# Mixing stage: whole-chunk scans with zeroed tile heads, and the ternary products in two exact passes

## The chip, the cores and the metric

The kernel runs on one core of a Trainium2 chip. The metric is the device time of one launch in microseconds (us). Five engines work side by side, each in its own order and tied by semaphores: PE (TensorE, matmuls and transposes into PSUM), ACT (ScalarE), DVE (VectorE), POOL (GpSimd) and SP, which only issues DMAs.

## The reference

Input `x` is 4 sequences of 1024 tokens with 256 channels, all in fp32. Three blocks follow one another: attention with 16 heads and a residual; a ternary feed-forward (layer norm, then a product with a weight rounded to -1, 0 or 1 and a scale); and a memory that is updated by gradient steps along the tokens, with a gate, and a second ternary feed-forward behind it. What matters here is how the memory's state runs over the tokens of a chunk of 128 tokens (in the kernel: a *tile*):

```
k, v, q = causal convolutions of four taps over projections of hidden
alpha, eta, theta = gates per token, means over 64 features
within each tile of 128 tokens, g from the state at the tile's start:
    S = eta[t] * S - theta[t] * g[t]
    W = (1 - alpha[t]) * W + S
ternary feed-forward: y = normalised(x) @ round_to_-1_0_1(w / scale) * scale
```

The recurrence is linear, so inside a tile it is written as four running sequences of factors, and each begins anew at a tile's first token. These four are the scans: `fz` (product of the etas, in the upper 64 partitions), `E` (eta times the former value minus the identity's column), `ab` (keep times the former value plus `fz`) and `C` (keep times the former value plus `E`), where keep is 1 - alpha.

## The kernel before, in words

Three stages run one after the other: projections and attention up to about 782 us of the profile's span, the *mixing* stage up to about 983 us, and the *memory* stage (`remember`) to the end. The change is in the mixing stage (`mix`), with small edits of buffers and one wait in the memory stage.

The mixing stage works on 8 chunks of 512 tokens (4 tiles of 128). It is a pipeline written out by hand: an iteration `it` from -4 to 7 does different steps for the chunks `it` to `it + 4`, and every engine walks its own fixed order of steps in each iteration:

- PE: projections of chunk it+1 (`projections`, L1244), ternary products of it+2 (`ffn_products`, L1181), gate means of it+1 (L1250), turning `z` of it+3 (`turn_z`, L1187), turning and multiplying keys of `it` (`key_products`, L1258 and L1264), gate products of it+1 (L1181), theta of it+1 (L1272), turning `hid` of it+2 (`turn_h`, L1187), attention output products of it+4 (`out_products`, L1181). The three L1181 groups share one helper, `token_products`: per chunk 8 products of 128x128 by 128x256, each of which the profile shows as two matmuls in fp32, so 16 rows. They share the two halves of one PSUM tile `ps_a`; `turn_z` and `turn_h` share `ps_t`.
- DVE: `add_out` of it+3 (L1103, with the moments L69 and L73), taps 1 and 2 of the convolution of `it` (L1134), `put_z` of it+3 (L81), tap 3 of `it`, `add_ffn` of it+2 (L1117, moments), `scan_decays` of `it` (the `fz` and `E` scans, L1146 and L1147, per tile), `put_h` of it+2 (L81), `scan_keeps` of `it` (the `ab` and `C` scans, L1081 and L1082, and four small copies L1087 to L1090), `products_of_keys` of `it` (L1095, tile `G`).
- ACT: copies of the projections of it+1 (L972 to L984), oldest taps (L998), log-sigmoid (L1003, behind a table load), `means` (eta L1010 and keep L1012), then the copy `zT` of it+3 out of `ps_t` (L1045), keys and values of `it` (L1029 to L1033), gates of it+1 (L1039), theta (L1018), the copy `hT` of it+2 (L1051).
- POOL: at the stage's start three clears (L940, L942) and ten clears of the memory stage's tiles (L951); in each iteration the deviations (L99 and L101), `divide_heads` of it+5 (L516), and the terms `aqb` and `kce` of `it` (L931 and L935).
- SP: loads of heads, stores of the terms; then it goes on with the memory stage's loads (L1387, L1394), the first of which wait for the last chunk's theta and for stored terms. `load_chain(1)` fills the second set of buffers.

Waits that matter: `out_products(n)` waits until the gates of chunk n-3 have left `ps_a`; `turn_h(n)` waits for `hid` of n and for the `zT` copy of n+1, since both use `ps_t`; `theta` waits for `keep`, since it writes over the means in PSUM; `gate_means` waits for the sigmoid L982. The last chunk's `ab` and `C` scans are left to the memory stage.

Of the kernel before, what the change touches and what calls it, by code (L numbers as in the profile page):

```python
# [795 lines left out]
Mix = namedtuple("Mix", ("on_sync on_gpsimd on_scalar on_vector on_tensor stored last_terms memory_terms scan_keeps products_of_keys pre sig_ea sig_t vT kce zT hT G aqb kv_c q_c eta keep ab C_ z hid ps_p ps_t ps_a states_zeroed th_ready f_ready gates_ready gate_ready th_taken hT_ready gate_taken g_ready kv_taken"))  # L796
# [3 lines left out]
def mix(ctx, nc, const, cols, oT, inverse, heads, x_all, gate_all, mem, states):  # L800
# [13 lines left out]
    hT, zT = two("hT", [P, CH, CHUNK]), two("zT", [P, CH, CHUNK])  # L814
# [123 lines left out]
    def on_gpsimd(pool):  # L938
        steps = Steps(pool, own_p)
        pool.memset(fz[LO], 0.0).then_inc(zeros_set, 1)  # L940
# [8 lines left out]
        pool.wait_ge(zeros_set, 3)  # L949
# [15 lines left out]
    def on_scalar(act):  # L965
# [87 lines left out]
        act.wait_ge(zeros_set, 3)  # L1053
# [43 lines left out]
    def on_vector(dve):  # L1097
# [43 lines left out]
        def scan_decays(n):  # L1141
# [8 lines left out]
        dve.wait_ge(zeros_set, 3)  # L1150
# [24 lines left out]
    def on_tensor(pe):  # L1175
# [42 lines left out]
        def turn_z(n):  # L1218
# [698 lines left out]
```

## Time and profile before

| | us |
|---|---|
| median of 3 runs (1185.11 to 1186.81) | 1186.75 |
| profiled execution, device time | 1184.83 |
| its span, first to last instruction | 1182.4 |
| PE busy, whole span | 1081.3 |
| DVE busy, whole span | 1006.6 |
| ACT busy, whole span | 804.2 |

The span is 2.4 us shorter than the device time of the same execution. Busy shares are means over stages with different limits, so the prediction reads the mixing stage alone, between 782 and 983 us. In a timeline each row is a start, a length, the engine, the line, the operation with its tiles and its count, and in brackets how long the engine had stood idle and what ended this.

### The profile page before, as it was taken

The page shows a single profiled execution, that of the slowest core. Times are in us where ns is not written, and L with a number is a line of the kernel's source. Part 1 is how long each engine was busy: PE and PEld are TensorE (multiplying, and loading weights), DVE is VectorE, ACT ScalarE, POOL GpSimd, SP SyncE. Part 2 cuts the span into 40 slices and gives each one's busy share as a digit, 9 for nine tenths or more (in the row PEclk, how much of TensorE's full clock was granted, in tenths as well). Part 3 has the DMA queues.
Part 4 walks back from the last instruction along what each step waited for, and adds up shares of the span by engine and source line. Part 5 has one row for each costly group of instructions (what it writes and reads, how often), then busy time and mean ns, then how long its engine had stood idle before and what let it go on. Part 6 is the DMA issues. An engine that isn't in the chain of part 4 may idle for free. (4 is left out here: it accounts for less than half of the span.)

```text
span 1182.4 us, 22162 instructions
## 1 busy us (share of the span) xinstructions
PE 1081.3 (91%) x8566; PEld 598.4 (51%) x8566; DVE 1006.6 (85%) x1591; ACT 804.2 (68%) x1628; POOL 229.2 (19%) x295
## 2 busy tenths in 40 slices
PE   5997799999999999999999999966999986989974
PEld 4884333333333333333333333345777755888864
DVE  7777999999999999999999999514799995488975
ACT  4461488888888888888888888931757673334431
POOL 6415100000000000000000000032333222556551
PEclk9997699999999999999999999988999996999996
DMA  7693313441442244134404400221233136433401
GB/s 270 155 353 132 55 28 58 65 61 25 73 66 46 40 73 65 32 54 65 65 22 72 73 20 12 74 82 58 63 125 136 67 122 179 131 112 100 131 19 53
DMA packets 87317, 101.56 MB, mean 86 GB/s; under 512 B 21868, under 2 KB 57196, under 8 KB 87212
## 3 DMA queue, kind: packets, MB, share of 16 engines
q1 hardware_dynamic: 86380, 98.56, 34.7%
q8 instruction: 67, 1.10, 0.4%
q10 hardware_dynamic: 832, 1.58, 0.4%
q14 instruction: 38, 0.31, 0.1%
HBM read 55.09 MB, written 43.88 MB: 84 GB/s over the span
## 5 line engine op out<-in xcount | busy, mean ns | idle before, releaser
L653 ACT ACTIVATE prob<-ps_s 128x512 f32<-128x512 f32 x1024 | 555.9, 597 | 114.6 <-PE ps_s L723 97.1
L674 DVE TENSOR_REDUCE maxes<-ps_m 128x2 f32<-128x1024 f32 x512 | 606.8, 1219 | 17.2 <-PE ps_m L712 13.7
L735 PE MATMUL ps_o<-prob,v_ones 128*32 128x256 f32 x4096 | 327.4, 391 | 7.8 <-issue 7.2
L723 PE MATMUL ps_s<-q_stack,k_stack 64*128 64x512 f32 x1024 | 261.5, 500 | 0.0
L712 PE MATMUL ps_m<-k_stack,q_stack 62*128 62x512 f32 x1024 | 218.9, 420 | 14.8 <-DVE maxes L674 11.1
L723 PEld LDWEIGHTS ps_s<-q_stack,k_stack 64*128 64x128 f32 x1024 | 99.5, 184 | 210.9 <-ACT prob L653 186.3
L735 PEld LDWEIGHTS ps_o<-prob,v_ones 128*32 128x32 f32 x4096 | 81.6, 108 | 192.1 <-issue 100.7
L712 PEld LDWEIGHTS ps_m<-k_stack,q_stack 62*128 62x128 f32 x1024 | 100.9, 192 | 31.6 <-DVE maxes L674 24.3
L615 POOL COPY v_ones<-v_all 128x512 f32<-128x512 f32 x16 | 9.9, 616 | 530.7 <-PE ps_o L735 530.7
L1103 DVE TENSOR_TENSOR x_all<-x_all,p_a 128x512 f32<-128x512 f32 x16 | 11.0, 685 | 49.9 <-PE p_a L1181 49.9
L69 DVE BATCH_NORM_STATS2 p_stats<-x_all 128x6 f32<-128x256 f32 x128 | 44.9, 413 | 6.1 <-DMA x_all<-in_x_dram 5.2
L405 ACT ACTIVATE p_parts<-ps_qk,cols 128x512 fp32r<-128x512 f32 x32 | 22.1, 689 | 36.9 <-PE ps_qk L450 35.2
L1244 PE MATMUL p_p<-p_hT,w_p 128*128 128x512 f32 x96 | 44.4, 614 | 2.2 <-ACT p_hT L1051 2.2
L516 POOL TENSOR_TENSOR heads<-heads,inverse 128x1024 f32<-128x1024 f32 x8 | 18.9, 2360 | 134.7 <-DMA inverse<-inverse_sums 134.7
L1181 PE MATMUL p_a<-w_out,heads 128*128 128x256 f32 x128 | 34.1, 428 | 3.2 <-PEq L524 3.2
L81 DVE TENSOR_SCALAR p_z<-x_all,p_mv,p_rstd 128x256 f32<-128x256 f32 x64 | 29.5, 522 | 8.2 <-POOL p_rstd L101 8.2
L324 DVE SCALAR_TENSOR_TENSOR p_parts<-ps_qk,cols,p_parts 128x512 fp32r<-128x512 f32 x32 | 23.6, 746 | 10.0 <-ACT p_parts L405 9.7
L1181 PE MATMUL p_a<-w_gate,p_hT 128*128 128x256 f32 x128 | 31.6, 403 | 0.0
L1181 PEld LDWEIGHTS p_a<-w_out,heads 128*128 128x128 f32 x128 | 27.5, 221 | 8.0 <-issue 3.7
L1244 PEld LDWEIGHTS p_p<-p_hT,w_p 128*128 128x128 f32 x96 | 18.6, 196 | 23.3 <-issue 20.3
L1181 PE MATMUL p_a<-ternary,p_zT 128*128 128x256 f32 x128 | 28.9, 379 | 0.0
L1181 PEld LDWEIGHTS p_a<-ternary,p_zT 128*128 128x128 f32 x128 | 24.3, 190 | 6.3 <-issue 3.3
(244 smaller groups left out, 1473.5 us busy)
## 6 DMA issues: line engine op xcount, KB each, us to landing
qk_parts<-p_parts SPq DMA_DIRECT2D x32, 512.0 KB, 7.4
q_stack<-qk_parts SPq DMA_DIRECT2D x96, 128.0 KB, 4.7
k_stack<-qk_parts SPq DMA_DIRECT2D x96, 128.0 KB, 7.7
oT<-o_sb SPq DMA_DIRECT2D x32, 256.0 KB, 4.0
x_all<-in_x_dram SPq DMA_DIRECT2D x8, 512.0 KB, 9.9
heads<-oT SPq DMA_DIRECT2D x16, 256.0 KB
inverse<-inverse_sums SPq DMA_DIRECT2D x16, 256.0 KB
out_dram<-x_all SPq DMA_DIRECT2D x8, 512.0 KB, 3.3
```

Source lines behind the costliest of these rows:

```text
L69: steps.did(dve.bn_stats(stats[:, i, :], src[:, i, :]))
L81: ins = dve.tensor_scalar(dst[:, i, :], src[:, i, :], mv[:, i, 0:1], rstd[:, i:i + 1], ALU.subtract, ALU.mult)
L324: dve.scalar_tensor_tensor(out=r32(parts[:, n % 2, j, 1]), in0=ps_qk[:, j], scalar=cols[:, COL_BQK + j:COL_BQK + j + 1], in1=parts[:, n % ...
L405: act.activation(r32(parts[:, n % 2, j, 0]), ps_qk[:, j], ACT.Identity, bias=cols[:, COL_BQK + j:COL_BQK + j + 1]).then_inc(hi_ready, 1)
L516: pool.tensor_tensor(o[:], o[:], heads["inverse"][n % 2][:], ALU.mult).then_inc(heads["divided"], 1)
L653: act.activation(prob[at % P_RING][:, h], ps_s[:, (GH * at + h) % S_RING], ACT.Exp, scale=HD ** -0.5).then_inc(exp_done, 1)
L674: dve.tensor_reduce(maxes[:, i // 2, i % 2], ps_m[:, i % M_PAIRS], AX.X, ALU.max).then_inc(m_taken, 1)
L712: ins = pe.matmul(ps_m[:, i // 2 % M_PAIRS, i % 2], r32(q_st[slot][base:base + MROW, hp, q0:q0 + P]), r32(k_st[slot][base:base + MROW, hp, ...
L723: pe.matmul(ps_s[:, (GH * (UNITS * slot + KT * qc + kt) + h) % S_RING], r32(k_st[slot][rows, pair, kt * P:(kt + 1) * P]), r32(q_st[slot][r ...
L735: ins = pe.matmul(ps_o[32 * h:32 * h + 32, queries], v_st[slot][:, kt, h], prob[(UNITS * slot + KT * qc + kt) % P_RING][:, h, queries], st ...
L1181: ins = pe.matmul(ps_a[:, i // 2, i % 2], src[:, c, i * P:(i + 1) * P], weights[:, c], start=c == 0, stop=c == CH - 1)
L1244: ins = pe.matmul(ps_p[:, j], w_p[:, c, j * P:(j + 1) * P], hT[n % 2][:, c], start=c == 0, stop=c == CH - 1)
```

## The change

It does five things.

1. The four scans run once per chunk, over 512 elements, instead of once per tile over 128. To start anew at each tile, the factor (eta or keep) is zero at the first token of each tile and the added term carries the start value there. `eta_first` (in rows of `pre_q` that were free) holds eta at the first tokens and zero elsewhere; `fz` in its lower half holds keep at the first tokens; `minus_idents` is the identity's negative four times. `fz` gets two buffers.
2. ACT writes eta and keep without their first columns, and these columns in an instruction each of their own.
3. The ternary products run as float32r: ACT writes `zT` rounded to it, DVE writes the rest into `zT_lo` (`lower_zT`), and PE multiplies both parts by the ternary weight into one sum. All waits for `zT` on PE become waits for `zT_lo`.
4. ACT copies `zT` before the log-sigmoid and the means; DVE does `fz`, then `lower_zT`, `put_h`, and only then `E`.
5. POOL clears and fills more tiles at the start, and the other engines wait for them. The memory stage takes the second `kce` and `vT` buffers and `zT_lo` from the mixing stage's tiles, and SP waits before `load_chain(1)` for the last chunk's `fz` scan.

```diff
+    hT, zT, zT_lo = two("hT", [P, CH, CHUNK]), two("zT", [P, CH, CHUNK]), sb("zT_lo", [P, CH, CHUNK])
+    E, fz, kT = sb("E", [P, CHUNK]), two("fz", [P, CHUNK]), sb("kT", [P, TPC, HALF])
+    eta_first, minus_idents = [tile[:, 0:CHUNK] for tile in pre[1]], sb("minus_idents", [P, TPC, MC])
+    ZEROS = 2 * 4 + TPC + 2
...
     def on_gpsimd(pool):
         steps = Steps(pool, own_p)
-        pool.memset(fz[LO], 0.0).then_inc(zeros_set, 1)
+        for s in range(2):
+            pool.memset(eta_first[s][HI], 0.0).then_inc(zeros_set, 1)
+        pool.wait_ge(zeros_set, 2)
+        for s in range(2):
+            pool.memset(fz[s][LO], 0.0).then_inc(zeros_set, 1)
+            for tile in (eta[s], keep[s]):
+                pool.memset(by_tile(tile[:])[:, :, 0:1], 0.0).then_inc(zeros_set, 1)
+        for i in range(TPC):
+            pool.tensor_copy(minus_idents[:, i], const["minus_ident"][:]).then_inc(zeros_set, 1)
...
-        pool.wait_ge(zeros_set, 3)
+        pool.wait_ge(zeros_set, ZEROS)
...
-            act.activation(eta[s][:], ps_p[:, 0], ACT.Copy, scale=0.9, bias=0.05).then_inc(gate_ready, 1)
+            act.activation(by_tile(eta[s][:])[:, :, 1:], by_tile(ps_p[:, 0])[:, :, 1:], ACT.Copy, scale=0.9, bias=0.05)
+            act.activation(by_tile(eta_first[s][HI])[:, :, 0:1], by_tile(ps_p[HI, 0])[:, :, 0:1], ACT.Copy, scale=0.9, bias=0.05).then_inc(gate_ready, 1)
...
-            act.activation(keep[s][:], ps_p[:, 1], ACT.Copy, scale=-0.1, bias=1.0).then_inc(gate_ready, 1)
+            act.activation(by_tile(keep[s][:])[:, :, 1:], by_tile(ps_p[:, 1])[:, :, 1:], ACT.Copy, scale=-0.1, bias=1.0)
+            act.activation(by_tile(fz[s][LO])[:, :, 0:1], by_tile(ps_p[LO, 1])[:, :, 0:1], ACT.Copy, scale=-0.1, bias=1.0).then_inc(gate_ready, 1)
...
-            act.activation(zT[n % 2][:], ps_t[:], ACT.Identity, scale=const["ternary_scale"][:]).then_inc(zT_ready, 1)
+            act.activation(r32(zT[n % 2][:]), ps_t[:], ACT.Identity, scale=const["ternary_scale"][:]).then_inc(zT_ready, 1)
...
             if valid(it + 1):
                 oldest_taps(it + 1)
+            if valid(it + 3):
+                copy_zT(it + 3)
+            if valid(it + 1):
                 log_sigmoid(it + 1)
                 means(it + 1)
-            if valid(it + 3):
-                copy_zT(it + 3)
...
-        for i in range(TPC):
-            c = slice(i * MC, (i + 1) * MC)
-            dve.tensor_tensor_scan(ab[s][:, c], keep[s][:, c], fz[:, i], const["ab_init"][:, 0:1], ALU.mult, ALU.add)
-            ins = dve.tensor_tensor_scan(C_[s][:, c], keep[s][:, c], E[:, i], 0.0, ALU.mult, ALU.add)
-        steps_s.did(ins)
+        dve.tensor_tensor_scan(ab[s][:], keep[s][:], fz[s][:], 0.0, ALU.mult, ALU.add)
+        steps_s.did(dve.tensor_tensor_scan(C_[s][:], keep[s][:], E[:], 0.0, ALU.mult, ALU.add))
...
-            for i in range(TPC):
-                c = slice(i * MC, (i + 1) * MC)
-                dve.tensor_tensor_scan(fz[HI, i], eta[s][HI, c], const["zeros"][HI], 1.0, ALU.mult, ALU.add)
-                ins = dve.tensor_tensor_scan(E[:, i], eta[s][:, c], const["minus_ident"][:], 0.0, ALU.mult, ALU.add)
-            steps_s.did(ins)
+            steps_s.did(dve.tensor_tensor_scan(fz[s][HI], eta[s][HI], eta_first[s][HI], 0.0, ALU.mult, ALU.add))
+
+        def scan_e(n):
+            steps_s.did(dve.tensor_tensor_scan(E[:], eta[n % 2][:], minus_idents[:].rearrange("p i t -> p (i t)"), 0.0, ALU.mult, ALU.add))
+
+        def lower_zT(n):
+            dve.wait_ge(zT_ready, n + 1)
+            if n:
+                dve.wait_ge(f_ready, 2 * n)
+            dve.scalar_tensor_tensor(out=r32(zT_lo[:]), in0=ps_t[:], scalar=const["ternary_scale"][:], in1=zT[n % 2][:],
+                                     op0=ALU.mult, op1=ALU.subtract).then_inc(zTlo_ready, 1)
...
             if valid(it):
-                scan_decays(it)
+                scan_f(it)
+            if valid(it + 3):
+                lower_zT(it + 3)
             if valid(it + 2):
                 put_h(it + 2)
+            if valid(it):
+                scan_e(it)
...
+        def ternary_products(k, n):
+            for i in range(2 * k, 2 * k + 2):
+                for j, rows_j in enumerate((zT[n % 2], zT_lo)):
+                    for c in range(CH):
+                        ins = pe.matmul(ps_a[:, i // 2, i % 2], r32(rows_j[:, c, i * P:(i + 1) * P]), r32(w_t[:, c]),
+                                        start=j == 0 and c == 0, stop=j == 1 and c == CH - 1)
+            ins.then_inc(f_ready, 1)
...
-                token_products(k, zT[n % 2], w_t, f_ready)
+                ternary_products(k, n)
...
             if valid(n + 1):
-                pe.wait_ge(zT_ready, n + 2)
+                pe.wait_ge(zTlo_ready, n + 2)
...
-    vT, kce, small = [m.vT[0], sb("vT1", [P, B, HALF])], [m.kce[0], sb("kce1", [P, B, P])], two("small", [P, B, 6])
+    vT, kce, small = [m.vT[0], flat(m.pre[1][1], B, HALF)], [m.kce[0], flat(m.pre[0][1], B, P)], two("small", [P, B, 6])
...
+            if c == 1:
+                sp.wait_ge(m.scan_steps, 3 * (NCH - 1) + 1)
```

## Rows read from the trace of the kernel before

**Rows 1.** Busy time by stretch; columns: us, PE, PEld, DVE, ACT, POOL, clock, DMA.

```profile
core 0: us, PE busy (x) PEld busy (x) DVE busy (x) ACT busy (x) POOL busy (x), PEclk, DMA share, GB/s
892.70:913.90 21.20, 21.20 (x102) 15.59 (x100) 20.33 (x57) 14.95 (x29) 8.23 (x8) 1.00 0.29 103
```

**Rows 2.** Timeline of PE: projections of chunks 1, 4 and 6, and one iteration.

```profile
840.98 5.31 PE L1244 MATMUL p_p<-p_hT,w_p 128*128 128x512 f32 x12
...
900.81 3.62 PE L1181 MATMUL p_a<-w_out,heads 128*128 128x256 f32 x16
904.26 5.31 PE L1244 MATMUL p_p<-p_hT,w_p 128*128 128x512 f32 x12
912.96 1.13 PE L1250 MATMUL p_p<-p_sig_ea,mean 64*128 64x512 f32 x4
...
944.14 5.42 PE L1244 MATMUL p_p<-p_hT,w_p 128*128 128x512 f32 x12 [1.11 <-ACT p_hT L1051]
```

**Rows 3.** Chain of work that ended last: ternary products here and in the memory stage.

```profile
909.57 3.45 PE p_a L1181 x16
...
1057.71 2.16 PE p_p L1510 x16
```

**Rows 4.** Timeline of ACT, same iteration.

```profile
896.46 1.11 ACT L1045 ACTIVATE p_zT<-p_t,ternary_scale 128x1024 f32<-128x1024 f32 x1
899.13 1.05 ACT L1039 ACTIVATE gate_all<-p_a 128x512 f32<-128x512 f32 x2
900.09 0.17 ACT L1018 ACTIVATE p_small<-p_p 128x4 f32<-128x4 f32 x1
907.90 0.69 ACT L976 ACTIVATE p_sig_t<-p_p,cols 64x512 f32<-64x512 f32 x1 [1.12 <-PE p_p L1244]
911.21 0.69 ACT L982 ACTIVATE p_sig_ea<-p_p,cols 128x512 f32<-128x512 f32 x1
```

**Rows 5.** Timeline of DVE, same iteration: scans.

```profile
894.72 0.75 DVE L1146 TENSOR_TENSOR_SCAN p_fz<-p_eta,zeros 64x128 f32<-64x128 f32 x1
895.48 0.42 DVE L1147 TENSOR_TENSOR_SCAN p_E<-p_eta,minus_ident 128x128 f32<-128x128 f32 x1
895.92 0.42 DVE L1146 TENSOR_TENSOR_SCAN p_fz<-p_eta,zeros 64x128 f32<-64x128 f32 x1
...
899.72 0.48 DVE L1081 TENSOR_TENSOR_SCAN p_ab<-p_keep,ab_init,p_fz 128x128 f32<-128x128 f32 x1
900.11 0.40 DVE L1082 TENSOR_TENSOR_SCAN p_C<-p_keep,p_E 128x128 f32<-128x128 f32 x1
900.43 0.46 DVE L1081 TENSOR_TENSOR_SCAN p_ab<-p_keep,ab_init,p_fz 128x128 f32<-128x128 f32 x1
...
904.46 0.69 DVE L1103 TENSOR_TENSOR x_all<-x_all,p_a 128x512 f32<-128x512 f32 x1 [0.27 <-PE p_a L1181]
```

**Rows 6.** Groups of DVE instructions, 850 to 1183 us; mean ns after the comma.

```profile
L1735 DVE TENSOR_TENSOR p_keep<-p_t,p_eta 128x512 f32<-128x512 f32 x6 | 4.2, 692 | 7.6 <-ACT p_eta L1567 7.6
L1702 DVE SCALAR_TENSOR_TENSOR p_zT_lo<-p_p,ternary_scale,p_zT 128x1024 fp32r<-128x1024 f32 x3 | 3.8, 1277 | 0.0
L1713 DVE TENSOR_TENSOR p_aqb<-p_p,p_G 128x256 f32<-128x256 f32 x6 | 2.5, 418 | 0.0
```

**Rows 7.** Timeline of POOL: stage's start and a division of heads.

```profile
782.87 0.52 POOL L940 MEMSET p_fz<- 64x512 f32 x1 [7.78 <-POOLq L524]
783.52 1.10 POOL L951 MEMSET p_ws<- 64x512 f32 x2
788.50 0.31 POOL L951 MEMSET w_o<- 64x256 f32 x1
790.82 0.20 POOL L99 TENSOR_TENSOR p_tmp<-p_mv,scalars 128x4 f32<-128x4 f32 x1 [2.01 <-DVE p_mv L73]
...
892.83 2.36 POOL L516 TENSOR_TENSOR heads<-heads,inverse 128x1024 f32<-128x1024 f32 x1 [4.59 <-DMA inverse<-inverse_sums]
```

**Rows 8.** Groups of POOL instructions, whole span.

```profile
L615 POOL COPY v_ones<-v_all 128x512 f32<-128x512 f32 x16 | 9.9, 616 | 530.7 <-PE ps_o L735 530.7
```

**Rows 9.** Timeline of PE, the stage's end.

```profile
960.54 1.09 PE L1187 MATMUL p_t<-ident,p_hid 128*128 128x128 f32 x8 [0.36 <-DVE p_hid L81]
962.75 7.11 PE L1244 MATMUL p_p<-p_hT,w_p 128*128 128x512 f32 x12 [1.11 <-ACT p_hT L1051]
972.23 1.13 PE L1250 MATMUL p_p<-p_sig_ea,mean 64*128 64x512 f32 x4 [2.37 <-ACT p_sig_ea L982]
974.23 2.07 PE L1264 MATMUL p_p<-p_q_c,p_kv_c 64*128 64x128 f32 x8
981.77 0.95 PE L1272 MATMUL p_p<-signed_mean,p_sig_t 128*128 128x1 f32 x8
```

**Rows 10.** Timeline of DVE, POOL and SP's queue, the stage's end.

```profile
976.49 0.68 DVE L1095 TENSOR_TENSOR p_G<-p_p,p_C 128x512 f32<-128x512 f32 x1
977.09 1.39 DVE L1134 SCALAR_TENSOR_TENSOR p_kv_c<-p_pre_kv,cols,p_kv_c 128x512 f32<-128x512 f32 x1
981.28 0.75 DVE L1134 SCALAR_TENSOR_TENSOR p_kv_c<-p_pre_kv,cols,p_kv_c 128x512 f32<-128x512 f32 x1
976.66 1.26 POOL L931 TENSOR_TENSOR p_aqb<-p_ab,p_q_c 128x512 f32<-128x512 f32 x1 [9.57 <-DVE p_small L1090]
983.92 0.56 SPq L1387 DMA_DIRECT2D p_kF<-m_kv  x1
```

More of the change, by code:

```diff
@@ L792 @@
 HALO = 3
-Mix = namedtuple("Mix", ("on_sync on_gpsimd on_scalar on_vector on_tensor stored last_terms memory_terms scan_keeps products_of_keys pre sig_ea sig_t vT kce zT hT G aqb kv_c q_c eta keep ab C_ z hid ps_p ps_t ps_a states_zeroed th_ready f_ready gates_ready gate_ready th_taken hT_ready gate_taken g_ready kv_taken"))
+Mix = namedtuple("Mix", ("on_sync on_gpsimd on_scalar on_vector on_tensor stored last_terms memory_terms scan_steps scan_keeps products_of_keys pre sig_ea sig_t vT kce zT hT G aqb kv_c q_c zT_lo eta keep ab C_ z hid ps_p ps_t ps_a states_zeroed th_ready f_ready gates_ready gate_ready th_taken hT_ready gate_taken g_ready kv_taken"))
 Remember = namedtuple("Remember", "on_sync on_gpsimd on_scalar on_vector on_tensor")
@@ L813, in mix @@
     o = heads["o"]
-    hT, zT = two("hT", [P, CH, CHUNK]), two("zT", [P, CH, CHUNK])
+    hT, zT, zT_lo = two("hT", [P, CH, CHUNK]), two("zT", [P, CH, CHUNK]), sb("zT_lo", [P, CH, CHUNK])
     z, hid = sb("z", [P, TPC, C]), sb("hid", [P, TPC, C])
@@ L844, in mix @@
     sums_moved, inverted = sem("sums_moved"), sem("inverted")
-    states_zeroed = sem("states_zeroed")
+    states_zeroed, zTlo_ready = sem("states_zeroed"), sem("zT_lo")
     own_z, own_h, own_c, own_s, own_p, passed = map(sem, (
@@ L854, in valid, with by_tile @@
         return 0 <= n < NCH
+    def by_tile(ap):
+        return ap.rearrange("p (i t) -> p i t", t=MC)
     def on_sync(sp):
@@ L1051, in copy_hT @@
             act.activation(hT[n % 2][:], ps_t[:], ACT.Copy).then_inc(hT_ready, 1)
-        act.wait_ge(zeros_set, 3)
+        act.wait_ge(zeros_set, ZEROS)
         for it in ITERATIONS:
@@ L1087, in scan_keeps @@
         dve.tensor_copy(small[s][:, :, 0:1], c_v[:, :, MC - 1:])
-        dve.tensor_copy(small[s][:, :, 1:2], E[:, :, MC - 1:])
+        dve.tensor_copy(small[s][:, :, 1:2], by_tile(E[:])[:, :, MC - 1:])
         dve.tensor_copy(small[s][:, :, 2:3], ab_v[:, :, MC - 1:])
-        dve.tensor_copy(small[s][:, :, 3:4], fz[:, :, MC - 1:]).then_inc(scanned, 1)
+        dve.tensor_copy(small[s][:, :, 3:4], by_tile(fz[s][:])[:, :, MC - 1:]).then_inc(scanned, 1)
     def products_of_keys(dve, n):
@@ L1139, in tap, with scan_f @@
                     ins.then_inc(conv, 1)
[L1141 removed]
+        def scan_f(n):
             s = n % 2
             dve.wait_ge(gate_ready, 2 * n + 2)
[L1144 to L1150 removed]
+            steps_s.did(dve.tensor_tensor_scan(fz[s][HI], eta[s][HI], eta_first[s][HI], 0.0, ALU.mult, ALU.add))
[7 more added lines that the diff above has]
+                                     op0=ALU.mult, op1=ALU.subtract).then_inc(zTlo_ready, 1)
+        dve.wait_ge(zeros_set, ZEROS)
         for it in ITERATIONS:
@@ L1199, in out_products @@
                 token_products(k, o[n % 2], w_out, w_ready)
+        def ternary_products(k, n):
[5 more added lines that the diff above has]
+            ins.then_inc(f_ready, 1)
         def ffn_products(n):
-            pe.wait_ge(zT_ready, n + 1)
+            pe.wait_ge(zTlo_ready, n + 1)
             for k in range(2):
@@ L1222, in turn_z @@
             elif n:
-                pe.wait_ge(zT_ready, n)
+                pe.wait_ge(zTlo_ready, n)
             turn(z, zT_turned)
@@ L1292, in on_tensor @@
                 out_products(it + 4)
-    return Mix(on_sync, on_gpsimd, on_scalar, on_vector, on_tensor, stored, last_terms, memory_terms, scan_keeps, products_of_keys, pre, sig_ea, sig_t, vT, kce, zT, hT, G, aqb, kv_c, q_c, eta, keep, ab, C_, z, hid, ps_p, ps_t, ps_a, states_zeroed, th_ready, f_ready, gates_ready, gate_ready, th_taken, hT_ready, gate_taken, g_ready, kv_taken)
+    return Mix(on_sync, on_gpsimd, on_scalar, on_vector, on_tensor, stored, last_terms, memory_terms, own_s, scan_keeps, products_of_keys, pre, sig_ea, sig_t, vT, kce, zT, hT, G, aqb, kv_c, q_c, zT_lo, eta, keep, ab, C_, z, hid, ps_p, ps_t, ps_a, states_zeroed, th_ready, f_ready, gates_ready, gate_ready, th_taken, hT_ready, gate_taken, g_ready, kv_taken)
 def remember(ctx, nc, const, rows, w, mem, x_all, gate_all, out, heads, start, m):
@@ L1337, in remember @@
     z, junk = m.z, m.hid
-    zT, zT_lo = sb("zT", [P, CH, B * P]), sb("zT_lo", [P, CH, B * P])
+    zT, zT_lo = sb("zT", [P, CH, B * P]), m.zT_lo
     norms, factor, ms = sb("norms", [P, 6, B]), sb("factor", [P, B]), sb("ms", [P, 3, B])
```

1 line of the change is left out of this document (removed).

## The prediction

> **What bounds the kernel now.** I read the busy time by stretch first. In a full iteration of the mixing stage PE is busy for all of its 21.20 us at full clock, DVE for 20.33, ACT for only 14.95 [rows 1]. The chain of waits agrees: from 850 to 943 us it is made of PE pieces that touch each other. So PE sets the period, and DVE has under 1 us of room. After that I read the timelines of the engines for one iteration, counted from P, the start of the projections (904.26) [rows 2], and last the end of the stage, where the chain changes to DVE and to SP's loads [rows 9, 10]. Four full periods count: the projections of chunk 1 start at 840.98 and those of chunk 4 at 904.26, 21.1 us a chunk, and those of chunk 5 follow one period later; the step to chunk 6 (944.14) takes only 18.7 us, since no output product is left there [rows 2].
>
> **Ternary products.** They take 3.45 us per chunk on the chain; the memory stage already does the same product in two float32r parts, 16 matmuls, in 2.16 us [rows 3]. PE alone would save 1.3 us a period. Not all of it is real, as three other engines' timings show.
>
> **A wait at the means.** ACT's sigmoid L982 ends at 911.21 + 0.69 = P+7.64 [rows 4]; the gate means start at P+8.70 now [rows 2] and would at P+7.40. With 0.05 for the hand-over PE waits to P+7.70, so 0.3 of the 1.3 is lost.
>
> **A wait at the output products.** From P+3.64 on (L976, 907.90) ACT is never idle until the gates are copied; the first gate copy begins at 899.13, in the next period P+16.07, and takes half of 1.05 or a little more, to P+16.65 [rows 4]. The output products begin at P+17.75 now (900.81 plus a period) [rows 2]; with the saving PE would be there at P+16.75. But ACT has two more instructions in front. The nearest rows are the 128x4 copies of 0.17 us, which can begin 0.1 after the one before [rows 4]; for both I take 0.3, with bounds of 0.1 and 0.6 (each as long as a short copy without overlap, and a strided large one a little longer). So the first gate copy is done at about P+16.95 and the output products, 3.45 long, end at P+20.4. Moving the `zT` copy (1.11 us) forward does not alter this sum; it delays `keep` to about P+14.7, just ahead of theta on PE (P+14.85).
>
> **DVE.** Here the trace shows only scans of 128 elements, so their price at 512 has to be bounded. From 692 ns at 512 and 418 ns at 256 elements a plain DVE instruction has 0.15 us that don't grow [rows 6]. With the same in a scan, 0.42 us at 128 leaves 2.1 ns an element, so 1.23 us at 512. A pair of `fz` and `E` takes 0.44 + 0.44 now, four pairs 3.5; the new pair is 0.88 + 2 x 0.81 = 2.5. A pair of `ab` and `C` takes 0.71 (899.72 to 900.43), four 2.9 with the settling; the new one 2.4 [rows 5]. That gives back 1.5 us. `lower_zT` adds 1.28 us, 1.20 from start to start [rows 6]. DVE's order without waits and disturbance is about 20.6 us now (21.20 less the wait of 0.27 and less 0.33 by which the first `fz` scan is longer than the others [rows 5]); it becomes 20.3. The bounds: if a scan has no fixed part, nothing comes back and DVE needs 21.8; if all that exceeds one element per 1.07 ns is fixed, 3.0 us come back and it needs 18.8. I take 20.3, by the rows of plain instructions.
>
> The Trainium skill, in "DVE: opcode table, instruction layouts, handler registers and perf-mode slots", section on datapath and trigger behaviour, says that this scan carries its result back through stages and runs at half throughput. No scan of another length is in the trace; at two cycles of 0.96 GHz an element the estimate from that page is 1.07 us plus the fixed part, which speaks against both bounds.
>
> **POOL beside DVE.** The long first `fz` scan (0.75 for 0.42) ends just behind POOL's division of heads, which runs until 895.19 [rows 5, 7]; DVE's two-input work on SBUF stands still beside it. In the new order the `fz` scan would come at P+11.4 and the division ends at P+12.1, so up to 0.65 us is lost unless DVE is late anyway. DVE's loop then lies between 20.3 and 20.9 and settles where its lateness uses up the disturbance, at 20.45 to 20.6. `hid` is ready at about P+15.9, since `E` now comes after `put_h`; PE wants it at P+15.7 to P+16. I take a period of 20.5, so 0.7 saved; four periods give 2.8 us. From chunk 5 to 6 nothing is gained: there ACT must first finish its gates and then copy `hT`, which ends at P+18.7, where it ends now.
>
> **The start.** POOL's clears grow from 0.65 us to about 3.6: four clears of 64x512 at 0.52, four strided and two small ones at 0.1, and four copies of 128x128 at 0.25 (a quarter of the 0.616 of a 128x512 copy would be 0.15, the whole would be 0.6) [rows 7, 8]. Then come the ten clears of the memory stage, 5.3 us, which now end at 788.81, 2.0 us before the first deviation is wanted (790.82) [rows 7]. PE and DVE stand behind that deviation. So 2.95 - 2.0 = 1.0 us is lost (bounds 0.6 and 2.4). In iterations -2 and -1 the chain runs over the loads of the heads, the division and `put_h`, so the shorter ternary products bring nothing, and theta of chunk 0 waits some 0.2 us for the later `keep`. Together +1.2.
>
> **The end.** Iteration 5 has no `lower_zT` and no output products: the ternary products of chunk 7 end 1.3 us earlier, DVE finishes their sum earlier and `hid` no longer waits behind `E`, so `turn_h` (960.54, waiting for `hid`) and the projections of chunk 7 (962.75) come some 1.45 earlier [rows 9]. From there DVE would be 4 us earlier, but its `G` of chunk 6 needs the key product, which ends at 974.23 + 2.07, only 0.2 before `G` starts at 976.49 [rows 9, 10]; so DVE's saving turns into a wait and 1.45 remains. It is partly used all the same: the taps behind `G` are slowed by POOL's `aqb` and `kce` (1.39 against 0.75 us for one) [rows 10], and with the scans over sooner POOL is done before the taps begin: 1.4 us. The memory stage's first loads also wait for theta of chunk 7, which ends at 982.72, 1.2 before the first load at 983.92 [rows 9, 10], so at most 1.1 of it counts. That is 2.5 us if PE's clock does as it does now. I take 2.8, for the case below. SP's new wait for the last `fz` scan ends 1.2 us behind the taps; `load_chain(1)` is issued 6 us after `load_chain(0)`, so it costs nothing; without this cover it would be 1.2. The shared buffers cost nothing: their last readers are the taps.
>
> **Sum.** +1.2 - 2.8 - 2.8 = -4.4 us, against the profiled execution 1184.8 to 1180.4. That execution lies 1.9 below the median of 1186.75; against the median the sum gives 1182.3.
>
> **The rivals.**
>
> *PE keeps its clock at the end.* The projections of chunk 7 take 7.11 us instead of 5.3, behind two idle gaps of PE (0.36 and 1.11) [rows 9]: the clock was at its lower level, 1.2 GHz, in part of them, and again in the key product (2.07 instead of 1.16). The first gap goes with the change. If the clock then stays at 2.4 GHz, the projections end 1.8 us earlier, the key product another 1 us; DVE and its taps become the limit, and the end gives 3.9 instead of 2.5: -5.5, 1181.2. The Trainium skill ("TensorE: Matmul & The Clock Gate", Part 1) says that the clock falls behind idle stretches and returns with sustained work; by that rule the shorter gap would favour this case. The gap of 1.11 stays, which speaks against it.
>
> *ACT or POOL's disturbance eats it.* Two short ACT instructions at 0.6 together, or a `fz` scan that always waits for the division, leave a period of 20.9 to 21.0: 4 x 0.25 = 1.0 saved, +1.2 at the start, -2.3 at the end: -2.1, 1184.6 to 1185.5. For it: ACT has no idle time in that stretch; against it: short copies overlap.
>
> *DVE becomes the bound (other side).* If a scan's cost is proportional to its length, DVE's order needs 20.6 + 1.2 = 21.8, with POOL in the way up to 22.1: +0.6 to +0.9 a period, +3.0, the start +1.2, at the end only the 1.3 of PE come back: +2.9, 1189.7. It decides from the point at which the scans give back less than 0.6 us of the 1.2 that `lower_zT` adds, at a fixed part under 0.05 us. Against it stands the fixed part of every other DVE instruction.
>
> *The products aren't faster here.* PE would pay 3.45 as now and gain nothing; speaks against: the same shape at the same clock in 2.16 [rows 3]. The time would be 1188.
>
> **Chances.** The forecast 0.48, the warm clock 0.16, the eaten gain 0.23, the DVE bound 0.10, slow products 0.03. A measurement of this kernel can tell a change of about 0.2%, 2.4 us. Faster by more than that: the first two nearly whole, 0.62; within it: the third and some of the first, 0.26; slower: 0.12. The forecast's own range is 1180.0 to 1184.8; to hold 8 in 10 I add the warm clock and full-rate scans below and the eaten gain above, 1179.0 to 1187.6.
>
> **What would show it.** Ternary products of 16 matmuls in 2.2 us; whole-chunk scans of 1.2 us; `lower_zT` of 1.28; a period of 20.5 between projections, PE idle for 0.3 before the means (released by the sigmoid) and a little before the output products (released by the gate copy); the first deviation at about 791.9; `G` of chunk 6 waiting for the key product. Scans of 1.6 us, a DVE without idle time and PE waiting for `hid` would show it wrong; so would a POOL start-up of over 5 us.

## The result, and the profile after

The changed kernel takes 1180.15 us (median of 5 runs, 1177.63 to 1181.09) beside 1186.81 us of the kernel before: a ratio of 0.9942, 95% interval 0.9927 to 0.9957, so 6.7 us less where 4.4 were forecast; against the median before, the forecast was 1182.3, and its own range began at 1180.0. The profiled execution took 1179.1 us with a span of 1176.4.

Beside each other, from PE's timeline of each profiled execution: S is the start of the output products of chunk 0, P1, P5, P6 and P7 the starts of the projections of these chunks, M the first product of the memory stage (us).

```
stretch                  before  after  after again  forecast
S to P1                   58.07  58.75        57.55      +1.2
P1 to P5 (4 periods)      84.31  81.11        81.10      -2.8
P5 to P6                  18.85  18.20        18.19       0
P6 to P7                  18.61  17.06        17.07      -1.45
P7 to M                   27.41  25.40        25.18      -1.35
M to the end             192.24 191.36       194.49       0
```

"After again" is the same kernel once more, with the third group of experiments. From P1 to M the two give the same to 0.3 us; in the first and the last stretch they differ by 1.2 and 3.1.

Busy time by stretch of the kernel after, two periods; columns as in [rows 1].

```profile
core 0: us, PE busy (x) PEld busy (x) DVE busy (x) ACT busy (x) POOL busy (x), PEclk, DMA share, GB/s
863.65:883.83 20.18, 19.71 (x101) 14.71 (x100) 19.65 (x46) 14.64 (x30) 8.91 (x9) 1.00 0.44 145
883.83:904.19 20.36, 19.76 (x101) 14.60 (x100) 19.83 (x46) 14.83 (x32) 9.28 (x9) 1.00 0.41 144
```

PE is no longer busy for the whole period: it now waits for ACT within it. The timeline of PE in the kernel after: the theta of chunk 0, the turning of `hid` in chunk 1's period, then one period and the stage's end:

```profile
838.02 1.02 PE L1306 MATMUL p_p<-signed_mean,p_sig_t 128*128 128x1 f32 x8 [1.25 <-ACT p_fz L1030]
...
859.26 1.09 PE L1213 MATMUL p_t<-ident,p_hid 128*128 128x128 f32 x8 [0.21 <-DVE p_hid L81]
...
883.83 5.31 PE L1278 MATMUL p_p<-p_hT,w_p 128*128 128x512 f32 x12
888.58 0.80 PE L1231 MATMUL p_a<-ternary,p_zT 128*128 128x256 f32 x2
889.22 0.40 PE L1231 MATMUL p_a<-ternary,p_zT_lo 128*128 128x256 f32 x2
...
890.64 0.39 PE L1231 MATMUL p_a<-ternary,p_zT_lo 128*128 128x256 f32 x2
891.52 1.13 PE L1284 MATMUL p_p<-p_sig_ea,mean 64*128 64x512 f32 x4 [0.49 <-ACT p_sig_ea L998]
...
900.66 3.69 PE L1207 MATMUL p_a<-w_out,heads 128*128 128x256 f32 x16
904.19 5.31 PE L1278 MATMUL p_p<-p_hT,w_p 128*128 128x512 f32 x12
...
942.58 5.42 PE L1278 MATMUL p_p<-p_hT,w_p 128*128 128x512 f32 x12 [1.47 <-ACT p_hT L1069]
959.64 5.42 PE L1278 MATMUL p_p<-p_hT,w_p 128*128 128x512 f32 x12 [1.11 <-ACT p_hT L1069]
967.43 1.53 PE L1284 MATMUL p_p<-p_sig_ea,mean 64*128 64x512 f32 x4 [2.37 <-ACT p_sig_ea L998]
...
969.93 2.07 PE L1298 MATMUL p_p<-p_q_c,p_kv_c 64*128 64x128 f32 x8
```

The ternary products are over at 891.03, P+7.20, where [rows 2] have P+8.70; the means then wait 0.49 for the sigmoid. The projections of chunk 7 take 5.42 instead of 7.11 [rows 9], the key product 2.07 as before. The chain of the kernel after (start, us, what) shows what that wait means: between projections and means it now runs over ACT's table load, the ACT_TABLE_LOAD in front of the sigmoid.

```profile
884.00 3.45 PE p_p L1278 x8
889.48 1.28 ACT L998
891.52 1.13 PE p_p L1284 x4
```

The timeline of ACT, kernel after, beside [rows 4]:

```profile
889.48 1.28 ACT L998 ACT_TABLE_LOAD   x1
890.78 0.69 ACT L998 ACTIVATE p_sig_ea<-p_p,cols 128x512 f32<-128x512 f32 x1
...
896.96 0.59 ACT L1026 ACTIVATE p_eta<-p_p 128x508 f32<-128x508 f32 x1
897.56 0.17 ACT L1027 ACTIVATE p_pre_q<-p_p 64x4 f32<-64x4 f32 x1
897.76 0.59 ACT L1029 ACTIVATE p_keep<-p_p 128x508 f32<-128x508 f32 x1
...
899.95 1.05 ACT L1057 ACTIVATE gate_all<-p_a 128x512 f32<-128x512 f32 x2
```

The timeline of DVE, kernel after, beside [rows 5, 10]:

```profile
854.66 1.94 DVE L1160 TENSOR_TENSOR_SCAN p_fz<-p_eta,p_pre_q 64x512 f32<-64x512 f32 x1
...
883.78 1.28 DVE L1119 TENSOR_TENSOR x_all<-x_all,p_a 128x512 f32<-128x512 f32 x2
...
895.56 1.22 DVE L1160 TENSOR_TENSOR_SCAN p_fz<-p_eta,p_pre_q 64x512 f32<-64x512 f32 x1
896.82 1.28 DVE L1169 SCALAR_TENSOR_TENSOR p_zT_lo<-p_t,ternary_scale,p_zT 128x1024 fp32r<-128x1024 f32 x1
898.02 1.38 DVE L81 TENSOR_SCALAR p_hid<-x_all,p_mv,p_rstd 128x256 f32<-128x256 f32 x4
899.31 1.22 DVE L1163 TENSOR_TENSOR_SCAN p_E<-p_eta,p_minus_idents 128x512 f32<-128x512 f32 x1
900.56 1.22 DVE L1098 TENSOR_TENSOR_SCAN p_ab<-p_keep,p_fz 128x512 f32<-128x512 f32 x1
901.70 1.20 DVE L1099 TENSOR_TENSOR_SCAN p_C<-p_keep,p_E 128x512 f32<-128x512 f32 x1
...
903.83 1.27 DVE L1119 TENSOR_TENSOR x_all<-x_all,p_a 128x512 f32<-128x512 f32 x2
...
972.04 0.69 DVE L1111 TENSOR_TENSOR p_G<-p_p,p_C 128x512 f32<-128x512 f32 x1 [0.28 <-PE p_p L1298]
972.65 1.01 DVE L1150 SCALAR_TENSOR_TENSOR p_kv_c<-p_pre_kv,cols,p_kv_c 128x512 f32<-128x512 f32 x1
```

The whole scans take 1.20 to 1.23 us where POOL isn't beside them (1.23 forecast), and DVE goes from one `add_out` to the next in 20.05 us without a wait. The timeline of POOL at the stage's start, kernel after, beside [rows 7]:

```profile
784.49 0.98 POOL L949 MEMSET p_pre_q<- 64x512 f32 x2 [6.16 <-POOLq L524]
...
787.71 1.10 POOL L967 MEMSET p_ws<- 64x512 f32 x2
...
794.03 0.20 POOL L99 TENSOR_TENSOR p_tmp<-p_mv,scalars 128x4 f32<-128x4 f32 x1 [1.03 <-DVE p_mv L73]
```

### The profile page after: what moved, and what is told of

It reads as the page before. It is cut to its first block and busy times, and to the rows that moved or that the text cites. A ratio compares the mean times of both kernels' runs of the same rounds, so it can differ in the third digit from the quotient of the medians.

```text
span 1176.4 us, 22108 instructions
## 1 busy us (share of the span) xinstructions
PE 1068.3 (91%) x8566; PEld 590.1 (50%) x8566; DVE 1003.4 (85%) x1503; ACT 805.0 (68%) x1644; POOL 235.5 (20%) x306
## 5 line engine op out<-in xcount | busy, mean ns | idle before, releaser
L99 POOL TENSOR_TENSOR p_tmp<-p_mv,scalars 128x4 f32<-128x4 f32 x24 | 12.6, 524 | 87.5 <-DVE p_mv L73 87.5
L1063 ACT ACTIVATE p_zT<-p_t,ternary_scale 128x1024 fp32r<-128x1024 f32 x8 | 8.8, 1106 | 27.9 <-PE p_t L1213 27.7
```

## The experiments

All are edits of the changed kernel unless said otherwise, and the diffs show the part that matters. There are three groups (the first four, the next four, the rest); the kernels of a group ran on one chip beside the kernel before, which took 1187.53, 1186.45 and 1188.09 us there. A ratio is to that kernel, with its 95% interval; across groups compare ratios, with 0.9942 for the changed kernel. A period is the time from one chunk's projections to the next chunk's.

**Tile scans.** The four scans cut back to 128 elements, in the new order.

```diff
-        dve.tensor_tensor_scan(ab[s][:], keep[s][:], fz[s][:], 0.0, ALU.mult, ALU.add)
-        steps_s.did(dve.tensor_tensor_scan(C_[s][:], keep[s][:], E[:], 0.0, ALU.mult, ALU.add))
+        for i in range(TPC):
+            c = slice(i * MC, (i + 1) * MC)
+            dve.tensor_tensor_scan(ab[s][:, c], keep[s][:, c], fz[s][:, c], 0.0, ALU.mult, ALU.add)
+            ins = dve.tensor_tensor_scan(C_[s][:, c], keep[s][:, c], E[:, c], 0.0, ALU.mult, ALU.add)
+        steps_s.did(ins)
```

> The changed kernel with its four scans cut back to 128 elements each (factors and order kept), 16 scans a chunk instead of 4. Theory A (the length counts, 0.15 us fixed per scan and DVE fully used): DVE's order grows by 1.5 us from 20.05 to about 21.5 a period, so the period becomes 21.5 and the time about 1180 + 4 x 1.2 + 1 to 2 at the end = 1186. Theory B (half of what a short scan cost before was not its fixed part but the change of starting partition between fz and E): scans of one kind in a row come every 0.32 to 0.36 us, DVE grows by 0.5 to 0.6, the period is 20.6 and the time about 1181.5. Theory C (PE and ACT set the period and DVE has room): 1180.5, period 20.3.

1181.70 us, ratio 0.9949 [0.9931, 0.9967]. Its timeline of DVE:

```profile
893.89 1.38 DVE L1165 TENSOR_TENSOR_SCAN p_fz<-p_eta,p_pre_q 64x128 f32<-64x128 f32 x4
...
899.19 0.42 DVE L1100 TENSOR_TENSOR_SCAN p_ab<-p_keep,p_fz 128x128 f32<-128x128 f32 x1
899.53 0.40 DVE L1101 TENSOR_TENSOR_SCAN p_C<-p_keep,p_E 128x128 f32<-128x128 f32 x1
```

From start to start the four kinds take 1.41 + 1.40 + 2.67 = 5.48 us a chunk; whole scans 4.88 (1.26 + 1.25 + 2.37), the kernel before 6.3 (3.4 + 2.9, undisturbed). So of the 1.4 us that DVE got back 0.8 came from the order and the start values inside the data, and 0.6 from the length. `fz` starts at partition 64 and `E` at 0: alternating they stood 0.44 apart [rows 5], four of a kind 0.35. The Trainium skill, "VectorE: DVE Perf Modes", section "Two Vector instructions with no wait between them", says that an instruction whose input starts in another quadrant than the last one read is held until all earlier ones are finished. The trace agrees: the alternating scans, 0.42 long, began only behind one another, those of a kind before the last had ended. DVE is as Theory B has it: its own order, from one `G` to the next, goes to 20.65. The first two periods are as before (20.36 and 20.19); in the later two PE waits 0.40 and 0.47 for `hid`, and they take 20.58 and 20.64. In time the 0.8 us can't be told from none.

**fp32 ternary products**, whole scans kept, `lower_zT` gone.

```diff
-                ternary_products(k, n)
+                token_products(k, zT[n % 2], w_t, f_ready)
```

> The changed kernel with the ternary products back in fp32: no lower_zT, 3.45 us on PE again, whole-chunk scans kept. Theory A (in full periods the gain is PE's, and scans alone bring nothing there): period 21.1 as before the change, PE without idle time, and only the end of the stage keeps some gain: about 1186.8 - 2 = 1185. Theory B (scans and products share the gain evenly): 1183.5. If shorter scans alone were enough: 1181.

1189.73 us, ratio 1.0012 [0.9996, 1.0029]; periods of 21.20 to 21.21, and P1 to M 149.5 where the kernel before has 149.2. Theory A for the periods; the 2 us it kept for the end aren't there. The whole gain hangs on PE's products; whole scans alone bring nothing.

**E ahead of hid.**

```diff
             if valid(it):
                 scan_f(it)
+            if valid(it):
+                scan_e(it)
             if valid(it + 3):
                 lower_zT(it + 3)
             if valid(it + 2):
                 put_h(it + 2)
-            if valid(it):
-                scan_e(it)
```

> The changed kernel with the E scan back in front of lower_zT and put_h. Theory A (hid is on PE's path since turn_h waits for it): hid comes 1.25 us later, PE waits about 1.0 us before turn_h, the period goes from 20.3 to 21.2 and the time to about 1184. Theory B (PE would wait for ACT's gate copy anyway, so the order on DVE is free): at most 0.2 us a period, 1180.5.

1184.39 us, ratio 0.9976 [0.9959, 0.9992]; periods of 20.77 to 21.00. PE waits for `hid` in each, as its timeline shows:

```profile
858.65 1.09 PE L1213 MATMUL p_t<-ident,p_hid 128*128 128x128 f32 x8 [0.59 <-DVE p_hid L81]
879.64 1.10 PE L1213 MATMUL p_t<-ident,p_hid 128*128 128x128 f32 x8 [0.82 <-DVE p_hid L81]
```

Moving 1.25 us of scan behind `hid` is worth 0.57 of the 0.8 us a period. By the ratios it is 4.0 us in time (0.9976 against 0.9942); the traces from P1 to M show 2.6 of it (144.35 against 141.77), and where the rest lies isn't shown.

**The copy of zT in its old place**, behind `keep`.

```diff
-            if valid(it + 3):
-                copy_zT(it + 3)
             if valid(it + 1):
                 log_sigmoid(it + 1)
                 means(it + 1)
+            if valid(it + 3):
+                copy_zT(it + 3)
```

> The changed kernel with ACT's zT copy back behind the log-sigmoid and the means. Theory A (the copy feeds lower_zT, which feeds put_h and turn_h): the copy ends 3.3 us later, lower_zT 1.5 us later, period about 21.5, time about 1185. Theory B (DVE can wait and catch up elsewhere): 1181.

1197.22 us, ratio 1.0079 [1.0058, 1.0100]: by the ratios 16 above the changed kernel, more than either theory. `lower_zT` waits 1.4 us for the copy on DVE (883.07, released by ACT L1063), `hid` stands behind it, and PE's timeline then shows:

```profile
885.69 1.46 PE L1213 MATMUL p_t<-ident,p_hid 128*128 128x128 f32 x8 [1.25 <-DVE p_hid L81]
886.95 4.98 PE L1207 MATMUL p_a<-w_out,heads 128*128 128x256 f32 x16
```

The output products take 4.98 instead of 3.62; the mean granted clock over this period is 0.93, so part of it ran at 1.2 GHz. In three of the first five periods the output products behind such a gap were slow (4.98 to 5.31), in two not (3.62). Periods of 21.45 to 23.46 are the wait and the clock together.

**No first columns.** ACT's two short instructions left out, and with them the right values of the first tokens.

```diff
-            act.activation(by_tile(eta_first[s][HI])[:, :, 0:1], by_tile(ps_p[HI, 0])[:, :, 0:1], ACT.Copy, scale=0.9, bias=0.05).then_inc(gate_ready, 1)
-            act.activation(by_tile(fz[s][LO])[:, :, 0:1], by_tile(ps_p[LO, 1])[:, :, 0:1], ACT.Copy, scale=-0.1, bias=1.0).then_inc(gate_ready, 1)
```

> The changed kernel without ScalarE's two short instructions on the first token of each tile (eta of the first tokens, keep of the first tokens); the values of these tokens in the E and fz scans are then not those of the reference, all else is as it was. Theory A (ScalarE's chain from the projections to the gates holds the output products back; my 0.3 us of the forecast): the out products wait for the gate copy 0.26 us less in every second period, the period goes from 20.28 to about 20.1, time about 0.4 to 0.7 us below the changed kernel (1179.5). Rival B (the period is set by the sigmoid that follows the products of the means and by VectorE's order of 20.05 us): the period stays 20.2 to 20.3 and the time within 0.3 us.

1179.27 us, ratio 0.9934 [0.9916, 0.9953]; four periods of 20.01 to 20.02. Its timeline of PE, the output products of chunk 3's period, 16.56 behind its projections (883.11):

```profile
899.67 3.62 PE L1205 MATMUL p_a<-w_out,heads 128*128 128x256 f32 x16
```

Theory A: the 0.27 us a period are what the two cost, and ACT's two halo copies in every second chunk (L1007, the last tokens of the chunk before, kept for the taps), which made 20.18 and 20.36 alternate, no longer show. In time the 1 us can't be told from none.

**Late clears.** POOL's ten clears of the memory stage behind the first deviation.

```diff
+            if it == -3:
+                pool.wait_ge(rstd_z, 1)
+                for k, tile in enumerate(states):
+                    pool.memset(tile, 0.0).then_inc(states_zeroed, 1)
```

> The changed kernel with GpSimd's clears for the memory stage moved behind its first deviation of the mixing stage, so that the clears of the two blocks' first tokens alone stand ahead of it. Theory A (the added clears delay the start, +1.2 in my sum): 0.8 to 1.2 us less. Rival B (TensorE at the lower clock decides when the first means are there, and GpSimd sat idle 1.03 us before its first deviation): start of the mixing stage to the projections of chunk 1 stays near 58.7 us, time within 0.3 us of the changed kernel.

1181.76 us, ratio 0.9960 [0.9943, 0.9976]. No gain, which speaks for Rival B, but its numbers are missed as well: the median lies 2 us above the changed kernel's by the ratios (the intervals overlap), and S to P1 takes 60.55 in the one trace, not 58.7. Its timelines of POOL and then of DVE:

```profile
791.92 0.20 POOL L99 TENSOR_TENSOR p_tmp<-p_mv,scalars 128x4 f32<-128x4 f32 x1 [5.09 <-DVE p_mv L73]
```

```profile
793.25 2.53 DVE L81 TENSOR_SCALAR p_z<-x_all,p_mv,p_rstd 128x256 f32<-128x256 f32 x4 [1.49 <-POOL p_rstd L101]
```

The deviation starts at S+8.2, when DVE's moments are there, against S+8.55 with the clears in front (the changed kernel once more, and the next kernel) and S+7.9 in the kernel before; and the clears now slow `z` beside them from 1.38 to 2.53.

**The table early.** A sigmoid of one column ahead of the wait for the projections, so that the table load falls into ACT's idle time.

```diff
+            act.activation(table_out[:], const["scalars"][:, S_ONE:S_ONE + 1], ACT.Sigmoid)
             act.wait_ge(p_ready, 3 * n + 1)
```

> The changed kernel with one more ScalarE instruction, a sigmoid of a single column ahead of the wait for the projections, so that the table for the sigmoid is loaded in ScalarE's idle time and not on the way from the projections to the gates. Theory A (after the change ScalarE's chain of sigmoid and gates is what holds TensorE: the means waited 0.49 us for the sigmoid in each period, the out products 0.26 in every second): both waits go, the period falls from 20.28 to VectorE's order of 20.05 or a little under, the chunks 5 to 7 and the end lose up to 1 us each, time 1176 to 1178. Rival B (the waits were the remainder of VectorE's order): waits move to hid or the product of theta, the period stays at 20.2 or above, time 1179 to 1180. Rival C (the table was loaded in idle time already): nothing changes.

1181.17 us (8 runs), ratio 0.9947 [0.9926, 0.9969], although the profiled run took 1174.9. Hence once more, beside the changed kernel:

> The changed kernel with the table for the sigmoid loaded in ScalarE's idle time, once more, since its trace was 4.2 us shorter than that of the changed kernel and its median of 8 runs was not. Theory A (the gain is real, and the medians were of chips and runs that differ in the granted clock): 1.5 to 3 us below the changed kernel beside it. Rival B (what the periods give, the idle stretches of TensorE and its clock take back elsewhere): within 0.5 us of it.

> The changed kernel itself once more, as the measure for the three beside it: 1179 to 1182, period 20.2 to 20.3, the means waiting 0.5 us for the sigmoid.

1183.18 us (9 runs), ratio 0.9953 [0.9933, 0.9973], against 1181.46 (6 runs, 1178.22 to 1184.31), 0.9941 [0.9924, 0.9957], which is the changed kernel's ratio over again. No gain, as Rival B has it. Both waits on ACT are gone in its traces, but PE's timeline (first of its executions, then, with DVE's row, the second) has new ones:

```profile
875.69 1.09 PE L1214 MATMUL p_t<-ident,p_hid 128*128 128x128 f32 x8 [0.41 <-DVE p_hid L81]
```

```profile
901.22 1.10 PE L1214 MATMUL p_t<-ident,p_hid 128*128 128x128 f32 x8 [1.11 <-DVE p_hid L81]
```

```profile
896.64 1.91 DVE L1161 TENSOR_TENSOR_SCAN p_fz<-p_eta,p_pre_q 64x512 f32<-64x512 f32 x1
```

DVE's order of 20.05 is the bound now, and the `fz` scan moves forward into POOL's division (895.12 to 897.48): periods of 19.65 to 20.30 in the first trace and 19.92 to 20.74 in the second. P1 to M takes 141.0 and 141.6 against 141.8 and 141.5: of the 1.1 and 0.4 us that four periods give, 0.2 to 0.5 goes again behind P5. There DVE's scans and taps are the limit (`G` of chunk 6 starts 12.9 us behind P7, not 12.4 or 12.2), and the taps stand longer beside POOL (5.6 us for 5.2 and 5.4).

**One pass.** The kernel leaves out the second of the two passes of the ternary products and `lower_zT`, and with them the low part of `z`.

```diff
-                for j, rows_j in enumerate((zT[n % 2], zT_lo)):
+                for j, rows_j in enumerate((zT[n % 2],)):
```

> [...] It takes another 2.2 us of TensorE and 1.28 us of VectorE out of each chunk. Theory A (after the change TensorE and VectorE aren't alone the bound, ScalarE's chain through the sigmoid is): period 20.0 to 20.2, time 1177 to 1179. Rival B (TensorE's products are the bound still, as before the change): period 18.5 to 19, time 1170 to 1173.

1179.60 us, ratio 0.9937 [0.9917, 0.9957]; periods of 20.36, 20.73, 20.36 and 20.19. Theory A's path, though three of the four periods lie above its 20.2; the 18.5 of Rival B is far off. Its timeline of PE:

```profile
881.64 5.31 PE L1276 MATMUL p_p<-p_hT,w_p 128*128 128x512 f32 x12
889.32 1.13 PE L1282 MATMUL p_p<-p_sig_ea,mean 64*128 64x512 f32 x4 [1.42 <-ACT p_sig_ea L998]
902.00 5.31 PE L1276 MATMUL p_p<-p_hT,w_p 128*128 128x512 f32 x12
```

The second pass is hidden: without it the means start at P+7.68, where they start with it (P+7.69), and wait 1.42 instead of 0.49. PE is ready 0.94 us earlier (P+6.26), which is what the pass is worth, and not 2.2. In the period of 20.73 the `fz` scan, earlier without `lower_zT`, falls into POOL's division (2.40 for 1.22), and PE waits 0.55 for `hid`.

**Last tokens on ACT.** The early table, and the four small copies behind the scans moved from DVE to ACT, all chunks but the last.

```diff
+            for j, src in enumerate((C_[s], E, ab[s], fz[s])):
+                ins = act.activation(small[s][:, :, j:j + 1], by_tile(src[:])[:, :, MC - 1:], ACT.Copy)
```

> The kernel with the early table, and ScalarE also makes the four copies of the last tokens of each chunk (C, E, ab, fz of the last token of each tile) in its idle time, which VectorE made behind the scans (0.08 us apart, about 0.35 us a chunk); the last chunk keeps them on VectorE. Theory A (with the table early VectorE's order of 20.05 us is the bound, and hid is what the products wait for): the wait for hid goes, the period falls from 20.0 to 19.65 to 19.75, which is TensorE's own sum, and the time by 1 to 2 us more: about 1176 if the changed kernel beside it gives 1180. Rival B: the period stays at 20.0.

1180.97 us, ratio 0.9938 [0.9922, 0.9954], not the 1176 of Theory A. Periods of 19.67, 20.18, 20.74 and 19.76: two of four are near 19.65, the shortest in any trace; in the others the `fz` scan meets the division. And P7 to M takes 27.05, 1.7 longer than in the kernel after and 0.8 longer than with the early table alone (26.23), as its timeline of POOL explains:

```profile
972.41 1.73 POOL L942 TENSOR_TENSOR p_aqb<-p_ab,p_q_c 128x512 f32<-128x512 f32 x1 [9.74 <-ACT p_small L991]
974.11 2.09 POOL L946 TENSOR_TENSOR p_kce<-p_kT,p_small 128x256 f32<-128x256 f32 x2
```

POOL waits for ACT, `kce` comes late, and SP's loads stand behind its store.

**The table early in the kernel before.** The same line, added there.

> The kernel before, with nothing but the early load of the table for the sigmoid. Theory A (before the change ScalarE's chain lay hidden under the longer ternary products; the means didn't wait): no change in the period of 21.1 to 21.2; at the end, where iteration 6 has no ternary products to hide it (the means of chunk 7 wait for the sigmoid), up to 1.2 us: 1185 to 1187. Rival B (the sigmoid was on the way in the periods too): period 20.8 or less, 1183 to 1184.

1186.76 us, ratio 0.9991 [0.9979, 1.0003]; periods of 21.03 to 21.04. Before the change ACT's chain lay under the longer products: the wait that the table load causes is one that the change uncovered. The means of chunk 7 wait 1.08 instead of 2.37.

## Why the prediction was right

The mechanism held; that the total fits is partly luck. 1180.15 lies 0.15 us inside the forecast's own range (1180.0 to 1184.8) and nearer to the rival of the warm clock (1181.2) than to the 1182.3 that was forecast. Behind P1 the change gave 7.4 us for the 5.6 that the sum has there, and how much the start took can't be read from two traces.

**Products: right.** They are over at P+7.20 (forecast P+7.40); with the table early, where nothing holds them, the means start at P+7.13, so they give 1.57 and not 1.3. Without the float32r passes nothing is gained.

**The wait at the means: right**, its end at P+7.69 (P+7.70), its length 0.49 (0.3), PE being earlier.

**The output products: right.** They start at P+16.83 here (forecast P+16.95) and at P+16.66 to 16.68 in periods without halo copies, behind the gate copy; without the two short instructions at P+16.56, and these cost 0.27 a period (0.3). The positions P+16.07, P+16.65, P+16.95 and P+17.75 of the forecast are each 0.17 too late, since a window of 21.20 was taken for a period of 21.03; corrected it reads P+16.78.

**DVE: the term that was mis-sized.** What scans and `lower_zT` change was right: 1.4 given back (1.5 forecast; four pairs of `fz` and `E` took 3.4, not 3.5), 1.20 added. But the sum started at "about 20.6 us now", and this should have been 20.25. From one `G` to the next DVE needed 21.0 us before, not the 21.2 of the window, and I took off one wait and one disturbance where about 0.2 more of waiting lay inside groups. So the order became 20.05 (20.25 - 1.4 + 1.2), not 20.3, and with the disturbance I added another 0.15 to 0.3 for a period of 20.5, set by DVE. Measured are 20.28, and DVE doesn't set them: after chunk 1 PE never waits for `hid`. Without any wait PE's own order would take 19.46, an estimate from 21.03 less 1.57; to this its waits for ACT add 0.56 before the means (P+7.13 to P+7.69), 0.10 or 0.27 before the output products and 0.07 within them, together 20.19 or 20.36. That makes -3.2 over four periods instead of -2.8. The division met the `fz` scan in chunk 1 (1.94 for 1.22) and cost PE 0.21 there, later almost nothing, as it ended at 895.28, just ahead of 895.56.

**Chunk 5 to 6: wrong, +0.65 us.** "There ACT must first finish its gates": ACT was free at 942.3 before and began the copy of `hT` at 943.07, released by PE's transposes, so PE set it, and shorter products do help. After the change ACT does set it: the copy follows its gates at once (941.51), and PE waits 1.47 for it instead of 1.11, which leaves 0.65 of PE's 1.0.

**The start: +1.2 isn't borne out.** S to P1 is 0.7 longer in one trace and 0.5 shorter in the other. POOL's clears grew by 2.6 us (784.49 to 787.71 against 0.65), not 2.95, and took 3.2 as against 3.6 forecast; of that 2.0 were covered. With DVE's moments ready at S+8.2 the loss is 0.35 us (S+8.55). In the profiled run after even that is hidden, since the output products of chunk 0 took 6.66 us at a granted clock of 0.55 where they took 5.08 at 0.72 before. The other part was too small: theta of chunk 0 waits 1.25 us for `keep` and its first columns, not 0.2, and from the projections of chunk 0 to those of chunk 1 it takes 19.80 in both traces where it took 19.45.

**The end: the -1.45 was right** (-1.55 from P6 to P7). P7 to M gave another 2.0 to 2.2 instead of 1.35, and by another path: 1.3 to 1.5 of it is that `G` of chunk 6 starts earlier behind P7 (12.4 and 12.2 us for 13.7), since the projections of chunk 7 took 5.42, at 2.4 GHz, as in the rival of the warm clock. The key product stayed at 1.2 GHz in one trace (2.07) and took 1.61 in the other, and `G` waited 0.28 for it in the first. The taps, for which the forecast had 1.4 (1.1 of it counted), gave 0.4 and 0.2: they still ran beside POOL (1.01 for the first). The end as a whole gave 3.6 and 3.8, nearer to the rival's 3.9 than to 2.8. In four other variants (tile scans, fp32 products, no first columns, one pass) it was the projections of chunk 6 that took 7.11 instead; the one with one pass had the same idle of 1.47 in front of them as the kernel after, with 5.42, so which product falls into the low clock is not explained by the last gap alone.

From P1 to M the change is worth 7.4 us (207.25 - 58.07 = 149.18 against 141.77, and 141.54 again). The medians give 6.7. What lies outside these marks varies from trace to trace: S to P1 takes 56.5 to 60.6 us in 13 of the 14 (62.0 with the late copy of `zT`), M to the end 191.2 to 195.6. The two traces of the same kernel show what goes with it; busy time by stretch, once and again:

```profile
985.00:1035.00 50.00, 41.50 (x288) 38.16 (x289) 22.54 (x66) 18.03 (x74) 24.59 (x32) 0.83 0.48 134
```

```profile
985.00:1035.00 50.00, 42.43 (x277) 39.35 (x276) 21.26 (x63) 18.02 (x74) 24.60 (x32) 0.78 0.41 117
```

The granted clock is 0.83 in one and 0.78 in the other (0.76 if the 50 us are counted from its M, 1.9 us earlier), right behind the mixing stage, and that execution's memory stage took 3.1 us longer. Why less is granted in one than in the other is open. For the same reason none of the variants can be called faster than the changed kernel.

## What to carry to other kernels

When the bound engine loses 1.3 us of 21, look at once for what is next, by its end and not by its share: here PE's 19.46 (the estimate above) stood under ACT's waits at P+7.7 and P+16.7, which make 20.28, and DVE's order of 20.05, so that taking away one of them (table, short copies) brought 0.3 us a period at most, and the second pass none. In an in-order queue the place of an instruction can be worth as much as its length: `E` ahead of `hid` cost over half the gain by the medians and a third by the traces, the copy of `zT` in its old place more than twice the gain. And count an engine's order from the same instruction to the same instruction, not over another engine's period.

## What the runs showed of the hardware

- Scans of 128 elements start 0.31 to 0.35 us apart when all start in the same partition and 0.44 when they alternate (partitions 64 and 0); one of 512 takes 1.22 us, 1.25 from its start to the next one's: four short ones cost 0.15 more for their number and 0.3 more for alternating.
- ACT's table load is 1.28 us; moved into idle time it brought the sigmoid's start from P+6.95 to P+5.66, that is by 1.29 and no more. The Trainium skill, "ScalarE: Activation LUTs", section "What ACT_TABLE_LOAD costs", gives 1.28 us for the load and about as much again for a drain; the trace has the first, and no room for the second.
- POOL's clears slow DVE instructions beside them (`z` 2.53 for 1.38, late clears), as its division of heads does (`fz` 1.94 for 1.22).
- Gaps of 1.25 to 2.63 us in front of PE's transposes (late copy of `zT`) were followed by products at 1.2 GHz in three cases of five; gaps of 0.6 to 1.1 us at the same place (`E` ahead of `hid`, early table) in none.
